# Odd states' C products in token layout on TensorE and ScalarE, and a woven feed-forward one head later from its gelu on

## What is computed

```python
def step(state, inp):                       # scan over the 256 tokens of each sequence
    d, b, c, u = inp
    dA = jnp.exp(d[..., None] * A)          # A: 256 channels x 16 states
    state = state * dA + (d * u)[..., None] * b[:, None, :]
    y = jnp.einsum('bdn,bn->bd', state, c)  # product with C, sum over the states
    return (state, y)
...
x = x + tanh(g_xattn[0]) * scan_block(ctx, layernorm(x))
x = x + tanh(g_ffn[0]) * mixture_of_64_experts(layernorm(x))
x = x + tanh(g_xattn[1]) * attention_16_heads(layernorm(x), ctx, mask)
# last feed-forward, per sequence
h = silu(bitlinear158(x, w1, b1)); h = gelu(h); h = layer_norm(h, ln_g, ln_b)
x = x + tanh(g_ffn[1]) * bitlinear158(h, w2, b2)
```

## Time and profile before

| | |
|---|---|
| median of 3 runs | 576.02 us (575.34 to 576.35) |
| the profiled execution's own time | 575.79 us |
| its span | 573.8 us (2.0 us lie around it) |
| PE, DVE, ACT, POOL busy | 84%, 82%, 64%, 49% of the span |
| mean granted TensorE clock | 0.955 of full speed |
| state stage, first scan to last | 44.13 to 159.4 us |
| experts, then attention | to 290 us, then 290 to 538 us |

### The profile page before, as it was taken

The page is one execution under the profiler, slowest core; times in us unless marked ns, Lnnn a source line. Parts: engine busy times, 40 slices in busy tenths (PEclk is TensorE's granted clock), DMA queues, the critical chain, the costliest instruction groups (busy, mean ns, idle before and its releaser), DMA issues.

```text
span 573.8 us, 10348 instructions
## 1 busy us (share of the span) xinstructions
PE 481.4 (84%) x3106; PEld 363.5 (63%) x3106; DVE 472.5 (82%) x1249; ACT 364.4 (64%) x831; POOL 279.7 (49%) x263
## 2 busy tenths in 40 slices
PE   6817777757889899999899999998699988998835
PEld 3302222222368766776888999987589888997714
DVE  4899999999997838788567857896899969875887
ACT  2785555435526555787676666679556796689544
POOL 4118777869520555630287368623874243333111
PEclk9956999999999999999899999999999999999876
DMA  5939400001045889893422012400335000000000
GB/s 155 228 84 324 125 0 1 1 1 37 1 136 154 272 256 295 233 306 104 167 58 63 1 38 57 56 2 1 53 57 61 0 2 2 19 2 1 0 20 19
DMA packets 45626, 48.63 MB, mean 85 GB/s; under 512 B 5660, under 2 KB 42118, under 8 KB 45574
## 3 DMA queue, kind: packets, MB, share of 16 engines
q1 hardware_dynamic: 41734, 36.46, 22.7%
q0 software_dynamic: 3840, 11.54, 9.1%
HBM read 41.43 MB, written 6.56 MB: 84 GB/s over the span
## 4 chain that ended last, share of the span: by engine, by line
PE 32%; DVE 23%; issue 22%; POOL 10%; ACT 7%; DMA 3%; SPq 1%; DVEq 1%; POOLq 0%; ACTq 0%
DVE hst L1884 7%; PE ps L1628 5%; PE ps L1567 3%; PE ps L1568 3%; PE ps L1569 3%; PE ps L1617 2%; POOL G L672 2%; POOL dbu L586 2%; POOL pn L688 2%; PE ps L1277 2%; PE ps L1485 2%; DVE hc L1893 2%; DMA G<-token_rows,idx_x 1%; POOL G L650 1%; PE ps L1521 1%
## 5 line engine op out<-in xcount | busy, mean ns | idle before, releaser
L688 POOL TENSOR_TENSOR pn<-pr,pinv 128x512 f32<-128x512 f32 x64 | 67.6, 1058 | 88.3 <-DVE pinv L2293 87.8
L586 POOL TENSOR_TENSOR dbu<-du,brow 128x512 f32<-128x512 f32 x64 | 81.3, 1282 | 41.6 <-DVE du L1877 23.1
L1277 PE MATMUL ps<-hc,ident 128*128 128x512 f32 x128 | 72.8, 657 | 27.2 <-DVE hc L1893 25.7
L1884 DVE TENSOR_TENSOR_SCAN hst<-ps,dbu 128x512 f32<-128x512 f32 x64 | 77.9, 1217 | 0.2 <-POOL dbu L586 0.2
L831 ACT ACTIVATE ps<-dtv,amat 128x510 f32<-128x510 f32 x64 | 44.1, 690 | 49.1 <-DVE hst L1884 48.2
L1019 ACT ACTIVATE pr<-ebuf,smin 128x256 f32<-128x256 f32 x128 | 63.7, 502 | 13.5 <-POOL pn L688 6.7
L1628 PE MATMUL ps<-pT,cS 128*128 128x256 f32 x256 | 66.5, 382 | 0.0
L1277 PEld LDWEIGHTS ps<-hc,ident 128*128 128x128 f32 x128 | 20.3, 195 | 66.9 <-DVE hc L1893 63.7
L650 POOL DMA_INDIRECT G<-token_rows,idx_x x32 | 37.7, 1179 | 44.2 <-DVE wkv L2019 20.8
L672 POOL DMA_INDIRECT G<-expert_out,idx_g x48 | 51.2, 1066 | 11.6 <-issue 10.7
L2284 DVE CUSTOM_DVE_ANT_0 ebuf<-ps,mbias 128x256 f32<-128x256 f32 x128 | 49.0, 420 | 5.9 <-issue 5.8
(11 more groups left out here) (380 smaller groups left out, 1384.3 us busy)
## 6 DMA issues: line engine op xcount, KB each, us to landing
wdn<-in_L_ffn_wd SPq DMA_DIRECT2D x12, 384.0 KB
wgu<-in_L_ffn_wg SPq DMA_DIRECT2D x11, 384.0 KB
wgu<-in_L_ffn_wu SPq DMA_DIRECT2D x11, 384.0 KB
expert_out<-xn SPq DMA_DIRECT2D x11, 256.0 KB
wq<-in_L_xattn_Wq SPq DMA_DIRECT2D x2, 1024.0 KB, 9.3
wo<-in_L_xattn_Wo SPq DMA_DIRECT2D x1, 2048.0 KB, 15.8
wo<-in_L_ffn_w SPq DMA_DIRECT2D x2, 1024.0 KB, 7.0
expert_out<-pexp SPq DMA_DIRECT2D x5, 256.0 KB
```

The lines of the kernel that those rows point to most:

```text
L586: nc.gpsimd.tensor_tensor(dbu[:, j, :], du[:, j % 2, 512 * hb:512 * hb + 512], brow[:, j // 2, :], ALU.mult).then_inc(pool_dbu, 1)
L688: nc.gpsimd.tensor_tensor(pn[:, h % 2], pr[:, h % 2], pinv[:, h % 2, :].unsqueeze(2).to_broadcast([P, 2, L]), ALU.mult)\
L1277: pe.matmul(bank(2 + j % 2), ident[:], hc[:, j % 2, :], start=(isinstance(m, int) and m + k == 0), stop=(isinstance(m, int) and m + k == N ...
L1884: V.tensor_tensor_scan(hst[:, j, :], bank(j % 2), dbu[:, j, :], 0.0, ALU.mult, ALU.add)\
```

## The change

In the state stage the odd state of each pair (j = 2, 3), but for the last pair of all, is no longer multiplied on DVE. PE transposes `hst[2]` and `hst[3]` (`turn_states`, twice four transposes, both halves into bank 7), ACT scales each transposed block by the C value of its token while it copies it to SBUF (`scale_turned`, four copies of 256 columns with a scale per partition), and PE transposes back by eight float32 products with the identity, which add into banks 2 and 3 (`turn_back`). `c_rows`, the C values with tokens on the partitions, come from 16 small products once, before the loop. DVE's order is scan 0, scan 1, product 0, scan 2, scan 3, product 1. Scans 2 and 3 wait until PE has read the states of the pair before. The routing steps are placed anew, and `lower_logits`, `logits_of` a little later.

In the attention, for f = 0 and 1, each step from the gelu on stands one slot later (gelu 13 to 14, variance 16 to 17, roots 15 to 16 and 17 to 18, quantising 18, 19 to 19, 20, transposes 20 to 21, product 22 to 23). `context_high` moves from h = 13 to h = 8, `context_low` from 13 to 14. SP waits for the C products before it loads Wq.

```diff
+            def scale_turned(hb, m, half):
+                pair = NS // 2 * hb + m
+                act.wait_ge(z_in_psum, 2 * pair + half + 1)
+                if half == 0:
+                    wait_count(act, y_added, 4 * pair if isinstance(pair, int) else 4 * pair + 1)
+                act.wait_ge(z_copied, 1)
+                for q in range(2):
+                    last = A((z_first, z_second)[half][:, q, :], bank(7)[:, DT * P * q:DT * P * q + DT * P], ACT.Copy,
+                             scale=c_rows[:, 4 * hb + 2 * half + q, bass.ds(2 * m + 1, 1)])
+                last.then_inc(z_copied, 1)
...
+                decay(hb, m, 0)
+                decay(hb, m, 1)
...
+                    scale_turned(*before, 0)
+                if not last:
+                    copy_b(*after, 0)
+                between(0)
+                decay(hb, m, 2)
+                if not first:
+                    scale_turned(*before, 1)
+                decay(hb, m, 3)
+                if not last:
+                    copy_b(*after, 1)
+                between(1)
...
+            def turn_states(hb, m, half):
+                pair = NS // 2 * hb + m
+                if half == 0:
+                    pe.wait_ge(scanned, 4 * pair + 4)
+                pe.wait_ge(z_copied, 2 * pair + half + 1)
+                for q in range(2):
+                    for d in range(DT):
+                        at = DT * P * half + P * q
+                        last = pe.transpose(bank(7)[:, DT * P * q + P * d:DT * P * q + P * d + P],
+                                            hst[:, 2 + d, at:at + P], ident[:])
+                last.then_inc(z_in_psum, 1)
+
+            def turn_back(hb, m, stop=False):
+                pair = NS // 2 * hb + m
+                pe.wait_ge(z_copied, 2 * pair + 3)
+                for d in range(DT):
+                    for c in range(4):
+                        done = pe.matmul(bank(2 + d)[:, P * c:P * c + P],
+                                         (z_first, z_second)[c // 2][:, c % 2, P * d:P * d + P], ident[:],
+                                         start=False, stop=stop and c == 3)
+                    done.then_inc(y_added, 1)
...
+                add_out(hb, m, 0, start=first)
+                if not late:
+                    turn_states(hb, m, 0)
+                add_out(hb, m, 1, start=first)
+                spread_c(*to_c, 0)
+                between(0)
+                turn_states(hb, m, 1)
+                if to_b:
+                    spread_b(*to_b, 0)
+                    spread_b(*to_b, 1)
+                turn_back(hb, m, stop=last)
+                between(1)
...
-                    if at == (15 if f < B - 2 else 14):
+                    if at == (16 if f < B - 2 else 14):
                         root_of(f, 1, 0)
...
-                    if at == 13 and f < B - 2:
+                    if at == 14 and f < B - 2:
                         gelu(f, 0)
                         gelu(f, 1)
```

More of the change, by code:

```diff
@@ L839, in copy_b, with take_c_rows, decays @@
                 A(brow[:, k, :], bank(4), ACT.Copy).then_inc(b_copied, 1)
-            def decays(hb, m):
-                for j in range(4):
-                    decay(hb, m, j)
-                    if j % 2:
-                        copy_b(hb, m + 1, j // 2)
+            def take_c_rows():
+                act.wait_ge(winT_in_psum, 4)
+                A(c_rows[:].rearrange("p c n -> p (c n)"), bank(7)[:, 0:NT * NS], ACT.Copy).then_inc(z_copied, 1)
+            def scale_turned(hb, m, half):
[8 more added lines that the diff above has]
+                last.then_inc(z_copied, 1)
+            def decays(hb, m, between):
+                before = divmod(NS // 2 * hb + m - 1, NS // 2) if isinstance(m, int) else (hb, m - 1)
+                after = divmod(NS // 2 * hb + m + 1, NS // 2) if isinstance(m, int) else (hb, m + 1)
+                first, last = isinstance(m, int) and hb + m == 0, isinstance(m, int) and hb and m == NS // 2 - 1
+                decay(hb, m, 0)
+                decay(hb, m, 1)
+                if first:
+                    take_c_rows()
+                else:
+                    scale_turned(*before, 0)
[9 more added lines that the diff above has]
+                between(1)
             def rows_turned(hb, k):
@@ L1252, in _ @@
                         .then_inc(dtraw_done, 1)
+            for c in range(NT):
+                for d in range(DT):
+                    last = pe.matmul(bank(7)[:, NS * c:NS * c + NS], u[:, d, P * c:P * c + P], xpT[:, d, NS:2 * NS],
+                                     start=(d == 0), stop=(d == 1))
+            last.then_inc(winT_in_psum, 1)
             pe.wait_ge(sel_ready, 1)
@@ L1397, in _, with state_pair @@
-            for n in range(NS - 4, 2 * NS):
-                hb, m, k = n // NS, n % NS // 2, n % 2
-                add_pair(hb, m, k)
-                if n + 2 < 2 * NS:
-                    spread_c((n + 2) // NS, (n + 2) % NS // 2, k)
-                if n + 4 < 2 * NS:
-                    spread_b((n + 4) // NS, (n + 4) % NS // 2, k)
-                if n == NS + 3:
-                    turn_out(0, 0)
-                if n == NS + 4:
-                    turn_out(0, 1)
-                if n == NS + 8:
-                    turn_normal(0, 0)
-                if n == NS + 10:
-                    turn_normal(0, 1)
-                if n == NS + 12:
-                    logits_of(0)
+            def state_pair(hb, m, to_c, to_b, between):
+                whole = isinstance(m, int)
+                late = whole and hb and m == 0
+                first, last = whole and m == 0, whole and m == NS // 2 - 1
+                if late:
+                    turn_states(hb, m, 0)
+                add_out(hb, m, 0, start=first)
+                if not late:
+                    turn_states(hb, m, 0)
+                add_out(hb, m, 1, start=first)
[7 more added lines that the diff above has]
+                between(1)
@@ L1414, in _ @@
+            spread_c(1, NS // 2 - 1, 1)
+            for j in range(4):
+                add_out(1, NS // 2 - 1, j, stop=(j > 1))
             pe.wait_ge(d_kv, 32)
```

227 lines of the change are left out of this document (128 added, 99 removed).

## The result

The changed kernel takes **594.0 us** (median of 4 runs, 592.2 to 595.6) against 575.7 for the kernel before on the same chip (4 runs): ratio 1.031, 95% interval 1.029 to 1.033. The profiled execution took 593.98 us, its span is 592.0, its mean granted clock 0.948. Forecast were 581.4 us, at most 587: slower is right, the size is not, by more than three times (+18.3 instead of +5.4).

A forecast was written before the change was run, and what follows sets the result against it. DVE was taken to set the state stage's pace, afterwards a PE-ACT ring. Ring 4.8, clock 1 and routing 2.6 made +8.4 us, feed-forward -3: +5.4 on 575.79, put at 581.4 us, range 575.5 to 587.

The forecast's parts named there:

- the ring: State stage: PE and ACT waiting on each other set the pace, one turn 7.22 us against 6.85 before; +4.8 us.
- The turn, 7.22 us: State stage: thirteen summed steps from one `turn_back` to the next, range 6.9 to 7.6 us; 13 turns x 0.37 us.
- rival 4: State stage: ring slower than summed through idle starts and half clock, turn 7.5 us, total 587 us; chance 0.12.
- The row: Profile row of eight float32 records in 1.06 us, 0.113 us apart, used to price `turn_back` at 1.81 us.
- rival 1: State stage: products overlap better than in the row, `turn_back` 1.34 us, turn 6.75, total 574 us; chance 0.08.
- The half clock, +1: First pairs of the state stage: one or two turns at the 1.2 GHz level; +1 us, ends 0 and +4.
- The routing, +2.6: Second half of the state stage: new routing costs 8.5 us instead of 5.9; +2.6, ends +0.5 and +5.
- The first two pairs: Start of the state stage: held by POOL's start in both kernels, so left out of the 13 counted turns.
- What follows the stage passes through: Behind the state stage: `sum_up(1)`, routing and experts hang on its end, so its delay passes through.
- Additions can't shrink: Bounds of the ring: additions and transposes can't shrink; one addition of product 0 stands in the turn at 0.86 us.
- Part 2, -3: Attention's feed-forward: f = 0 gains 3 of the gathers' 4.3 us, f = 1 nothing; ends -4.3 and +2.
- rival 3: Attention: part 2 gives nothing or costs, as the root behind three gathers makes DVE late; 584 to 586 us, chance 0.22.

The follow-up runs named there:

- the fill: Changed state stage with the old feed-forward, plus six unused 512-column bf16 products on PE per pair of the first half: 591.0 us, 1.022.
- the third trial: Changed state stage, old feed-forward, B spread before second transposes, first transposes before first addition, ACT waiting for 4 x pair additions; then second scaled copies before decay: 586.2 us, 1.015.
- the state stage alone: The state stage's part of the change with the feed-forward where it stood before: 596.0 us, 1.033 of the kernel before.

## Why the prediction was right and wrong

- **Direction and mechanism: right.** DVE is no longer the limit, and the ring between PE and ACT is (turn 7.49 summed, 7.50 from scan to scan). Each of its conditions was in the sum; DVE's idle time is ended by ACT's decays, as said.
- **The turn, 7.22 us: 0.27 too short.** `turn_back` took 1.88 instead of 1.81, and the first transposes with the hand-over to ACT 0.87 instead of 0.72; the rest agrees to 0.05 each. A turn is 0.65 longer than before, not 0.37: over six loop turns 3.9 us, and rival 4 (7.5) had the right number. The row was the right price, and rival 1 is out. By the figure in the section "Back-to-back issue gap" of the Trainium skill's "TensorE: Matmul & The Clock Gate" `turn_back` would be 1.30 us, an estimate; the trace disagrees with its 1.88.
- **The half clock, +1: the step that failed.** I took the low clock for a thing of the start and never asked whether it would come back once PE waits in a ring. It did: three times in the first half, 4.95 us, and twice in the second, 1.65 and about 1.5, together some 8 of the 18.1 us; the sum had nothing for them. With the fill the first half had none. The Trainium skill, "TensorE: Matmul & The Clock Gate", section "A second HAM failure mode: psum-queue depth-cycling", tells of a kernel whose clock swings since PE idles briefly between groups of products. The run with the fill agrees with that; the third trial, whose PE idles nearly as much and whose clock stayed up, shows that it isn't enough for a forecast.
- **The routing, +2.6: its terms were not too small; a stretch was left out.** To the last scan 5.2 us stood in the sum, the ring's 7 turns or 2.6 and the routing's 2.6; without the two falls of the clock 3.3 are measured there. (The 5.9 us of routing before were also taken too low: eight whole pairs were taken off a stretch that ends with a scan. By the pairs' lengths it is 6.4, and the +2.6 would have been +2.1.) What failed is that the sum ends at the last scan: behind it 3.05 us more passed until the sums, with the logits ahead of the last products and PE's queue there. So the second half's 9.6 are 3.3, 3.05 and about 3.2 of the clock.
- **The first two pairs.** The first pair got faster (5.95 against 6.55), the second slower (7.85 against 6.90): together +0.35, inside the +1 with its ends of 0 and +4. This is luck in part: the second pair, with the same program, took 7.15 us in the trace of the state stage alone, in which the start's low clock ended 1.7 us earlier and the next fall came only at 79 us. The first scan came 1.0 later, though the C products were to hide. Without the change it lay between 44.1 and 45.2 us, so this is not more than its scatter.
- **What follows the stage passes through: held, as far as the traces tell.** Of 19.8 us at the sums 1.9 are gone at slot 3, but by the comparison above that is within what the clock and the scatter of this stretch make.
- **"Additions can't shrink" is true and led me astray:** they can leave the path. In the order with B spread first they lie beside ACT's copy; I summed PE's queue as fixed in the program's order, and did not look for the one line in it that ACT waits for.
- **Part 2, -3: wrong in its second sequence.** f = 0 came to -2.27, near the forecast, but with luck: in the three other traces in which it has the same place (51.01, 50.60 and 50.96 us) the clock fell near its long slot and left 0.2 to 0.6 of the gain. That f = 1 "gains nothing" held, but it lost 2.05: I looked at ACT's work for the moved steps, and not at what stands in the slot to which DVE's quantising moves. Net -0.2. In sum that is rival 3, part 2 giving nothing, but by another mechanism than its late root.
- By terms of the text: first half +0.35 and six turns 3.9 and the clock 4.95, makes 9.2; second half 9.6; first scan 1.0; sums to slot 3 -1.9; attention +0.2; rest +0.05. With the rounding that is 18.1, the difference of the spans.

## What to carry to other kernels

When work leaves a full engine for two others that hand it to each other, write the new ring down and ask of each instruction in it who waits for it: the one that others wait for (here one spread of B) goes ahead of those that nobody waits for (two additions). PE's order was worth 21 us here (from 1.033 to 0.9956 of the kernel before), more than the 17.4 us of products that DVE lost; in the traces of these two kernels it is 17 us from first scan to last, about 5 of them falls of the clock that didn't come or cost nothing. Where PE comes to wait in every turn, give the low clock a term in the loop as well, not only at the start, with a wide range; and of a step moved by one slot, list what already stands in the new slot on each engine.

## What the runs showed that I had not expected

- The granted clock fell to the 1.2 GHz level in the middle of a steady loop, for about 3 us, in some turns and not in others with the same instructions: pairs of 7.50 and of 9.15 us stand side by side. With additional products that nobody needs, PE did more, the falls in this loop were gone, and the kernel's median was 5 us lower. How many falls an execution has differs for the same program: three and two in the two traces of this loop.
- A hand-over between PE and ACT costs little: from the last transpose's or spread's end to ACT's start 0.13 to 0.27 us, from ACT's end to PE's start 0.05.
- A wait that shrinks in the trace (5.2 to 2.4 us for one addition) moved the slot by 0.2 us only, since DVE, the engine behind both waits, had hardly any idle time (6.50 of 6.50 and 6.79 of 7.00 us).
- An idle time in a profile can be a missing record: 2.12 us in front of PE's products were 0.87 and 0.86 around one product whose weight load alone was recorded. Comparing the counts of weight loads and products on the page shows it.
